# Attention scores in 64-row tiles of the array, with two-bank units for the row maxima, in a macaron layer

## The reference

```python
x = x + 0.5 * _L0_ffn_ref(_layernorm(x), ...)     # its own small attention and 2 of 8 experts
x = x + _L0_attn_ref(_layernorm(x), ...)          # 16 heads of width 8, causal, over all 2048 tokens
x = x + 0.5 * _L0_ffn_ref(_layernorm(x), ...)
```

```python
att = jnp.einsum('bhqd,bhkd->bhqk', q, k) / scale
att = jnp.where(causal, att, -jnp.inf)
att = softmax(att, axis=-1)
y = jnp.einsum('bhqk,bhkd->bhqd', att, v)
```

## Time and profile before

| | us |
|---|---|
| median of 3 runs | 2124.73 |
| lowest, highest | 2117.54, 2128.99 |
| span of the profiled execution | 2118.6 |
| busy: TensorE matmul, VectorE, ScalarE, GpSimd | 1699.8, 1403.2, 1071.9, 375.2 |

### The profile page before, as it was taken

The page is one execution under the profiler, slowest core; times in us unless marked ns, Lnnn a source line. Parts: engine busy times, 40 slices in busy tenths (PEclk is TensorE's granted clock), DMA queues, the critical chain, the costliest instruction groups (busy, mean ns, idle before and its releaser), DMA issues. The chain is left out here.

```text
span 2118.6 us, 30151 instructions
## 1 busy us (share of the span) xinstructions
PE 1699.8 (80%) x10502; PEld 714.0 (34%) x10502; DVE 1403.2 (66%) x2898; ACT 1071.9 (51%) x2292; POOL 375.2 (18%) x425
## 2 busy tenths in 40 slices
PE   3489999999708945699999998367999999971695
PEld 1223333333305732233333332122333333321474
DVE  7588999986222346688999982566899898713133
ACT  1145677677504422155777668113466777761342
POOL 4200101000052333000202010230001011004332
PEclk9679999999858977699999999667899999995798
DMA  2600012500011132400202300151002022000112
GB/s 86 155 2 2 9 40 75 117 12 1 1 34 43 43 106 74 96 1 2 46 2 46 52 2 2 55 146 24 2 2 47 2 50 47 2 1 25 44 42 80
DMA packets 76362, 85.70 MB, mean 40 GB/s; under 512 B 10167, under 2 KB 71164, under 8 KB 74520
## 3 DMA queue, kind: packets, MB, share of 16 engines
q1 hardware_dynamic: 71656, 75.14, 14.6%
q0 software_dynamic: 4544, 8.47, 1.2%
HBM read 53.11 MB, written 31.38 MB: 40 GB/s over the span
## 5 line engine op out<-in xcount | busy, mean ns | idle before, releaser
L721 ACT ACTIVATE probs<-ps 128x512 f32<-128x512 f32 (+3 forms) x1920 | 885.1, 540 | 546.8 <-PE ps L830 544.8
L586 DVE TENSOR_REDUCE mpart<-ps 128x1 f32<-128x512 f32 (+3 forms) x1680 | 1018.7, 667 | 167.9 <-PE ps L784 122.3
L784 PE MATMUL ps<-ka,qa 96*128 96x512 bf16 (+3 forms) x1920 | 667.2, 368 | 40.8 <-DVE ps L567 28.2
L830 PE MATMUL ps<-qa,ka 96*128 96x512 bf16 (+3 forms) x1920 | 632.3, 357 | 72.6 <-DMA qa<-guard 49.2
L843 PE MATMUL ps<-probs,vv 128*9 128x512 f32 (+3 forms) x3840 | 443.2, 534 | 1.8 <-POOL probs L673 1.8
L673 POOL TENSOR_SCALAR_AFFINE_SELECT probs<-probs 128x512 f32<-128x512 f32 x192 | 121.9, 635 | 1308.5 <-ACT probs L721 1308.5
L784 PEld LDWEIGHTS ps<-ka,qa 96*128 96x128 bf16 x1920 | 191.4, 100 | 469.5 <-DVE mpart L586 315.6
L830 PEld LDWEIGHTS ps<-qa,ka 96*128 96x128 bf16 x1920 | 183.4, 99 | 308.1 <-ACT probs L721 145.1
L1104 DVE SCALAR_TENSOR_TENSOR probs<-probs,arena,ps 128x448 f32<-128x448 f32 x78 | 53.1, 681 | 213.0 <-PE ps L1044 213.0
L787 PE MATMUL ps<-mask_rows,identb 128*128 128x128 bf16 x768 | 158.6, 231 | 0.0
L738 PE MATMUL ps<-identf,onat 128*128 128x128 f32 x48 | 15.6, 450 | 122.4 <-DVE onat L528 122.4
(11 more groups left out here) (149 smaller groups left out, 1075.1 us busy)
## 6 DMA issues: line engine op xcount, KB each, us to landing
qa<-qsplit SPq DMA_DIRECT2D x27, 384.0 KB
ka<-ksplit SPq DMA_DIRECT2D x27, 384.0 KB
sent<-padrow SPq DMA_DIRECT2D x3, 2535.0 KB, 15.7
probs<-rope SPq DMA_DIRECT2D x3, 2048.0 KB, 9.4
arena<-sent SPq DMA_DIRECT2D x78, 65.0 KB, 1.8
arena<-results SPq DMA_DIRECT2D x16, 256.0 KB, 4.6
qsplit<-arena SPq DMA_DIRECT2D x9, 384.0 KB, 4.1
ksplit<-arena SPq DMA_DIRECT2D x9, 384.0 KB, 2.6
```

Of the source, the lines that this page charges most:

```text
L586: dve.tensor_reduce(mpart[:, j % MD, h0:h0 + some, qt, kc], ps[:, bank, 0:some * w].rearrange("p (h w) -> p h w", h=some), axis=AX.X, op=A ...
L721: act.activation(probs[:, s % 2, h, 0:n], ps[:, u % SB, 0:n], ACT.Exp, scale=SCALE).then_inc(probs_ready, 1)
L784: ins = pe.matmul(dst, qa[0:KROWS, b, h0 + k, tile * 128:(tile + 1) * 128], ka[0:KROWS, b, h0 + k, kc * CH:kc * CH + n], start=True, stop= ...
L830: pe.matmul(dst, ka[0:KROWS, b, h, kt * 128:(kt + 1) * 128], qa[0:KROWS, b, h, c * CH + q0:(c + 1) * CH], start=True, stop=True).then_inc( ...
```

## The change

Four things are done together.

- The operands of a head take 64 rows instead of 96. Even heads of a group lie on partitions 0 to 63, odd heads on 64 to 127, so that a pair of heads sits in the two row halves of the array. Eight of the nine products of parts are in `qa` and `ka`; the ninth, that of the two smallest parts, and the three guard rows lie in a second pair of tensors, `qx` and `kx`. A row maximum uses the first pair of tensors alone. A score is two matmuls that add up in one bank, and a pair of heads is issued together: four matmuls into two banks, behind one wait.
- A rowmax unit covers a pair of heads in two adjacent banks, and one reduction on VectorE takes both. There are two such double banks, three banks for scores as before, and one accumulator for values.
- VectorE copies the turned maxima to SBUF; GpSimd makes the three parts. The memsets of guard rows fall away.
- Operands are loaded by 16 DMAs where 6 were, and the guard is read back by two where one was. The planner's constants follow.

```diff
-KROWS = 96
-GUARD = 9 * HD
+NP = HPG // 2
+HALF = 64
+GUARD = HD
...
-SB, MB = 3, 3
+SB, MB = 3, 2
+ACC = SB + 2 * MB
...
-            units += [(j, qt, h, 1, kc) for h in range(HPG) for kc in range(c)]
-            some = min(HPG, TPC // (qt + 1))
-            units += [(j, qt, h, some, c) for h in range(0, HPG, some)]
+            units += [(j, qt, p, 1, kc) for p in range(NP) for kc in range(c)]
+            some = min(NP, TPC // (qt + 1))
+            units += [(j, qt, p, some, c) for p in range(0, NP, some)]
...
-            dve = max(dve, pe + hop) + 1000
-            banks[bank] = dve - 400 + hop
-            ready[j] = dve + 5500
+            dve = max(dve, pe + hop) + 300
+            banks[bank] = dve + hop
+            ready[j] = dve + 7500
...
-            for h in range(HPG):
-                u = HPG * s + h
-                main(max(exp_at.get(u - SB, 0.0) + hop, ready[j]), n / 2.4 + 3, j)
-                act = max(act, pe + hop, values_at.get(s - 2, 0.0) + hop) + 52 + n * 0.83
-                exp_at[u] = act
-                events.append(("scores", s, j, kt, h))
+            for p in range(NP):
+                u = HPG * s + 2 * p
+                main(max(exp_at.get(u + 1 - SB, 0.0) + hop, ready[j]), 2 * n / 2.4 + 6, j)
+                for k in (0, 1):
+                    act = max(act, pe + hop, values_at.get(s - 2, 0.0) + hop) + 52 + n * 0.83
+                    exp_at[u + k] = act
+                events.append(("scores", s, j, kt, p))
...
-        b, heads, rows = g % 2, slice(g * HPG, (g + 1) * HPG), 3 * HD
-        for r in range(3):
-            for src, at, dst in ((qsplit, 0, qa), (ksplit, r * HD, ka)):
-                sp.dma_start(dst[r * rows:(r + 1) * rows, b, :, cols],
-                             src.rearrange("l (i h) t -> (l i) h t", h=H)[at:at + rows, heads, cols]
-                             ).then_inc(done, 16)
+        b, rows = g % 2, 3 * HD
+        qs = qsplit.rearrange("l (i g p o) t -> (l i) g o p t", g=NG, o=2, p=NP)[:, g]
+        ks = ksplit.rearrange("l (i g p o) t -> (l i) g o p t", g=NG, o=2, p=NP)[:, g]
+        for o in (0, 1):
+            at = HALF * o
+            for r, n in ((0, rows), (1, rows), (2, HALF - 2 * rows)):
+                first = (r + 1) % 3 * HD
+                sp.dma_start(qa[at + r * rows:at + r * rows + n, b, :, cols], qs[0:n, o, :, cols]).then_inc(done, 16)
+                sp.dma_start(ka[at + r * rows:at + r * rows + n, b, :, cols],
+                             ks[first:first + n, o, :, cols]).then_inc(done, 16)
+            sp.dma_start(qx[at:at + HD, b, :, cols], qs[2 * HD:3 * HD, o, :, cols]).then_inc(done, 16)
+            sp.dma_start(kx[at:at + HD, b, :, cols], ks[2 * HD:3 * HD, o, :, cols]).then_inc(done, 16)
...
                         if j >= MD:
-                            sp.wait_ge(guard_ready[j % MD], 16 * (j // MD))
+                            sp.wait_ge(guard_ready[j % MD], 32 * (j // MD))
 
                         sp.dma_start(guard[j % MD].rearrange("l r t -> r l t"), m3[:, j % MD, :, :]).then_inc(guard_stored[j % MD], 16)
                         sp.wait_ge(guard_stored[j % MD], 16 * (j // MD + 1))
-                        sp.dma_start(qa[GUARD:GUARD + 3, g % 2, :, c * CH:(c + 1) * CH],
-                                     guard[j % MD].rearrange("l (h q) t -> l h (q t)", h=HPG)).then_inc(guard_ready[j % MD], 16)
+                        for o in (0, 1):
+                            at = HALF * o + GUARD
+                            sp.dma_start(qx[at:at + 3, g % 2, :, c * CH:(c + 1) * CH],
+                                         guard[j % MD].rearrange("l (p o q) t -> l o p (q t)", p=NP, o=2)[:, o]
+                                         ).then_inc(guard_ready[j % MD], 16)
...
-                        sp.wait_ge(guard_zeroed, ev[1] + 3)
+                        sp.wait_ge(scores_ready, group_end(ev[1]))
...
-                        dve.tensor_reduce(mpart[:, j % MD, h0:h0 + some, qt, kc],
-                                          ps[:, bank, 0:some * w].rearrange("p (h w) -> p h w", h=some),
+                        dve.tensor_reduce(mpart[:, j % MD, 2 * p:2 * (p + some), qt, kc].rearrange("p (k o) -> p o k", o=2),
+                                          ps[:, bank:bank + 2, 0:some * w].rearrange("p o (k w) -> p o k w", k=some),
                                           axis=AX.X, op=ALU.max).then_inc(filler_used, 1)
...
-                            dve.wait_ge(guard_ready[j % MD], 16 * (j // MD))
-                        src = ps[0:16, bank, 0:128]
-                        link(dve.tensor_copy(m3[:, j % MD, 0, :], src))
-                        dve.tensor_tensor(mr, src, m3[:, j % MD, 0, :], ALU.subtract).then_inc(filler_used, 1)
+                            dve.wait_ge(guard_split, j - MD + 1)
+                        dve.tensor_copy(mraw[:, j % MD, :], ps[0:16, bank, 0:128]).then_inc(filler_used, 1)
                         dve.wait_ge(filler_used, mi)
-                        link(dve.tensor_copy(m3[:, j % MD, 1, :], mr))
-                        dve.tensor_tensor(m3[:, j % MD, 2, :], mr, m3[:, j % MD, 1, :],
-                                          ALU.subtract).then_inc(guard_split, 1)
+                        dve.engine_nop().then_inc(maxima_copied, 1)
...
-                        pool.wait_ge(scores_ready, group_end(ev[1]))
-                        pool.wait_ge(masked, TPC * NC * (ev[1] + 1) + TPC)
-                        pool.memset(guard_rows(ev[1] % 2), 0.0).then_inc(guard_zeroed, 1)
-                        pool.wait_ge(guard_zeroed, ev[1] + 3)
+                    elif ev[0] == "maxout":
+                        j = ev[1]
+                        pool.wait_ge(maxima_copied, j + 1)
...
+                        pool.tensor_copy(m3[:, j % MD, 0, :], raw).then_inc(maxima_parts, 1)
+                        pool.wait_ge(maxima_parts, 3 * j + 1)
+                        pool.tensor_tensor(mr, raw, m3[:, j % MD, 0, :], ALU.subtract).then_inc(maxima_parts, 1)
+                        pool.wait_ge(maxima_parts, 3 * j + 2)
+                        pool.tensor_copy(m3[:, j % MD, 1, :], mr).then_inc(maxima_parts, 1)
+                        pool.wait_ge(maxima_parts, 3 * j + 3)
+                        pool.tensor_tensor(m3[:, j % MD, 2, :], mr, m3[:, j % MD, 1, :],
+                                           ALU.subtract).then_inc(guard_split, 1)
+                        pool.wait_ge(guard_split, j + 1)
...
                         for k in range(some):
-                            dst = ps[:, bank, k * n:(k + 1) * n]
-                            ins = pe.matmul(dst, qa[0:KROWS, b, h0 + k, tile * 128:(tile + 1) * 128],
-                                            ka[0:KROWS, b, h0 + k, kc * CH:kc * CH + n], start=True, stop=not diag)
-                            if diag:
-                                ins = pe.matmul(dst[:, n - 128:n], identb[:, :], mask_rows[:, :],
-                                                start=False, stop=True)
+                            for o in (0, 1):
+                                rows = slice(HALF * o, HALF * (o + 1))
+                                ins = pe.matmul(ps[:, bank + o, k * n:(k + 1) * n],
+                                                qa[rows, b, p0 + k, tile * 128:(tile + 1) * 128],
+                                                ka[rows, b, p0 + k, kc * CH:kc * CH + n],
+                                                start=k == 0, stop=not diag)
+                        if diag:
+                            for k in range(some):
+                                for half in (0, 1):
+                                    for o in (0, 1):
+                                        rows = slice(HALF * o, HALF * (o + 1))
+                                        ins = pe.matmul(ps[:, bank + o, (k + 1) * n - 128:(k + 1) * n],
+                                                        identb[rows, half, :], mask_rows[rows, half, :],
+                                                        start=False, stop=half == 1 and k == some - 1)
...
-                            pe.wait_ge(guard_ready[j % MD], 16 * (j // MD + 1))
+                        if kt == 0 and p == 0:
+                            pe.wait_ge(guard_ready[j % MD], 32 * (j // MD + 1))
                         q0 = max(0, kt - TPC * c) * 128
                         n = CH - q0
-                        u = HPG * s + h
-                        if u >= SB:
-                            pe.wait_ge(probs_ready, u - SB + 1)
-                        dst = ps[:, u % SB, 0:n]
-                        pe.matmul(dst, ka[0:KROWS, b, h, kt * 128:(kt + 1) * 128],
-                                  qa[0:KROWS, b, h, c * CH + q0:(c + 1) * CH],
-                                  start=True, stop=True).then_inc(scores_ready, 1)
+                        u = HPG * s + 2 * p
+                        if u + 1 >= SB:
+                            pe.wait_ge(probs_ready, u + 1 - SB + 1)
```

(64 more changed lines are left out.)

55 lines of the change are left out of this document (30 added, 25 removed).

## The result

The changed kernel takes 2241.95 us in the median of four runs (2240.06 to 2244.91) where the kernel before took 2122.82 beside it: a ratio of 1.0565, 95% interval 1.0535 to 1.0594. It is slower by 119 us; the forecast was slower by 31, with a range that ends at 2235.

The account below looks back on a forecast made before the run. TensorE was taken as the bound, with VectorE close behind. Lead-in, early, dense and tail terms sum to 3 x (10 - 10 + 4 + 6) + 1.5 = +31.5 us, giving 2156 us, with a range of 2075 to 2235.

Parts of the forecast that it names:

- Overlap of the row halves: TensorE's row maxima: both halves run at once, 0.36 us a step less; partial overlap 7%, none 5%.
- VectorE's relief: VectorE in the attention stage: fewer reduction units save 18 us a pass, the smaller split of maxima 14.
- The loop: Scores and exponentials, a pair waiting for two of three banks: a full step takes 2.88 us, now 2.44.
- the tail: Last stretch of the stage, without row maxima: 58 us where it takes 52 now, +6 a pass.
- the dense floor: Dense stretch at ScalarE's loop alone, without hits from rowmax units: 299 us, -2 a pass.
- Units in the way: Rowmax units met when a pair falls due in the dense stretch: 6 us a pass, between nothing and 34.
- the dense term: Dense stretch of the stage: loop of 299 us plus 6 for rowmax units, 305, +4 a pass.
- Lead-in: Stretch until the first exponential: later guard from added DMA issues, +10 us a pass, between 0 and +14.
- Early stretch: Stretch after the lead-in, where row maxima bind: -10 us a pass, between 0 and -22.
- setup: Outside the stage, six selects at the start: 1.5 us once.
- The Trainium skill's figure for four row tiles: Row halves: 3.07 times for four tiles, as efficiency 1.5 times for two, hence partial overlap at 2260 us; chance 7%.

Follow-up runs that it names:

- e11: The changed kernel with VectorE splitting the maxima into three parts again, in place of GpSimd; 2238.84 us, 1.055 of the kernel before.
- e1: The changed kernel without all rowmax units but the last of each chunk; 2150.7 us in one run.
- e2: The changed kernel with the planner putting a filler unit ahead of a matmul only if TensorE would wait there; 2199.75 us, 1.0361 of the kernel before.
- e10: The kernel before with each operand DMA cut into two of two heads, same bytes; 2135.2 us, 1.0056 of the kernel before.
- e12: The changed kernel with seven products in one matmul a score, group 1 loaded behind the first guard, fillers only where TensorE waits or maxima are urgent; 2017.07 us.
- e4: The changed kernel without the second matmul of each score, its product and the guard; 2156.3 us in one run.
- e3: The changed kernel with SyncE issuing group 1's operand DMAs after the first guard's read-back; 2202.97 us, 1.0357 of the kernel before.

## Why the prediction was wrong

The mechanism was right, and so was the direction: TensorE's relief is real and goes into waiting, because the loop of scores and exponentials takes its place. One term of the sum was far too small.

- *Overlap of the row halves*: right, in full; no partial loss.
- *VectorE's relief*: 32 us a pass expected, 32.5 measured (busy in the stage's windows, 374.6 to 342.1). The counts of units in a group should read 16 x 6 + 4 x 11 and 8 x 6 + 4 x 6; the totals of 560 and 288 hold. I had VectorE below the loop in the dense stretch, rightly; e11 shows that its part from the split is worth nothing.
- *The loop*: right in its step. Tail step 2.88 worked out, 2.87 measured, with waits of 0.49 and 0.21 in it in place of 0.37 twice; group without units 107 worked out, 105.8 in e1. Against the kernel before, the loop alone costs 8.8 us from chunk 3 on (365.0 to 356.2), where I had +6 for the tail and -2 for the dense floor: 5 more than forecast.
- *Units in the way*: **this step failed.** I put 6 us a pass into the dense term "as between two pairs TensorE is free for 0.93 us and holds two units there", with 34 as the upper bound. The runs show 27 (392.4 to 365.0), and the dense window is 331 us long where I had 305. The place is there, but the list doesn't use it: the planner's loop calls for a unit before it asks whether TensorE would wait, so it puts one before the first pair in 101 of 160 steps and before the values in 65. The line is the same in the kernel before, and so in kind is its list (133 and 58 steps); TensorE was full there, and what the order costs in that kernel no run shows. The code was in front of me, and I argued from what it could do. e2 shows it: the same work with the test first brings the group to 106.2, and the time from chunk 3 on to 371.4, with the late guard of the last chunk in it. This term is 21 us a pass, 64 of the 88 by which I was short. Most of the rest is the loop's 5 us a pass, 8 by which the first two passes lost more than the third, and some 4 outside the stage.
- *Lead-in*: +10 forecast, +15.8 measured. SyncE reaches the guard 27.7 us after the memset, near the 30 implied, though group 1's block is longer than I had it: the trace has 32 issues from 1510.41 to the guard's store, where the kernel before has 12 from 1418.88, so 20 were added there and not 10. But the store then waits 17.6 us, where I had about 9 with the data drained at 151 GB/s. Windows of 5 us in the changed kernel against the earlier trace rows:

```profile
1525.00:1530.00 5.00, 0.00 (x0) 0.00 (x0) 0.00 (x0) 0.00 (x0) 0.00 (x0) 0.50 0.79 118
1530.00:1535.00 5.00, 0.00 (x0) 0.00 (x0) 0.00 (x0) 0.00 (x0) 0.00 (x0) 0.50 0.77 94
```

  The number of DMAs alone doesn't do it: e10, with twice as many as before, moved 163 and 157 GB/s in the windows from 1440 to 1450 us. What else slows them, such as their fewer rows, no run separates.

- *Early stretch*: -10 forecast, -15.9 measured, so the two errors cancel. What shortens it is not settled: with the guard first the chunks 0 to 2 end at 115.8 in the changed kernel and 115.6 in the one before, without it at 129.9 and 130.0. VectorE's split has at most 1 us of it.
- *Outside the stage* nothing but setup was counted. SyncE's longer queue also holds up ScalarE ahead of the memset: in pass three it waits 4.47 us for the store of q's parts, where it waited 2.54 for GpSimd at the same place before. The stage accounts for 36 to 42 us a pass, 116 in all, and some 6 lie outside it.

The Trainium skill's figure for four row tiles ("TensorE: Matmul & The Clock Gate", Measured speedup vs the span model) as an efficiency for two would have given 2260, close to the measured time, for a reason that the trace refutes: the halves take 0.39 together, and the next pair starts 0.23 later, so two row halves lose nothing here. That estimate would have been right by luck.

## What to carry to other kernels

When an engine is relieved, look for the chain that takes its place and lay it out from one step of the tail; here that gave 2.88 us against 2.87. Then ask of every piece of filler where the list really puts it and not where there would be room, because on a chain a misplaced piece counts, here with some 0.2 us each. And a matmul split in two in series lengthens a chain of matmul and exponential by its streaming time, here 0.44 us a step, though it costs the array nothing when two halves run at once.

## What the runs showed of the hardware

- Two 64-row matmuls on the two halves of the array, 512 columns into two banks, start together and take the time of one (0.39 us, the next pair 0.23 later), while VectorE reads other banks. With 56 and 59 rows it is the same (0.39 in e12).
- In e4 the granted clock fell to 0.50, the 1.2 GHz level, early in the last chunk, after the short steps at the end of chunk 14, in which TensorE was busy for 3.02 of 5 us:

```profile
1885.00:1890.00 5.00, 3.02 (x32) 1.10 (x29) 0.00 (x0) 4.01 (x12) 1.27 (x2) 0.86 0.00 0
1890.00:1895.00 5.00, 4.73 (x20) 1.42 (x18) 1.24 (x3) 1.79 (x5) 0.00 (x0) 0.50 0.00 0
```

  ScalarE had 1.79 us of work in the 5 us at that level, after 4.01. The last chunk took 41.7 us with a step of 2.43, where the kernel before took 37.6 with one of 2.44. What made the clock fall is not shown: the same loop, with TensorE busy for 3.38 of 5 us, stayed at 1.00 from 1900 to 1910 us, and so did the changed kernel's whole tail.
- A 12 KB store issued behind group 1's 2.36 MB on SyncE's queue took 16.3 us before and 17.6 in the changed kernel, and 1.5 ahead of them (e3). The same bytes in the changed kernel's DMAs, some of them with fewer rows, moved at 118 and 94 GB/s late in the drain in place of 151; cut in two by heads (e10) they moved at 163 and 157.
